# TensorE's certain expert turns written out, their gathered tiles transposed in place

## The reference

```python
logits = x @ router_w + router_b
topv, topi = jax.lax.top_k(logits, TOP_K)              # 2 of 8 experts
topw = jax.nn.softmax(topv, axis=-1)
h1 = jnp.einsum('bsd,edf->ebsf', x, W1) + b1[:, None, None, :]   # 128 -> 512
h2 = jnp.einsum('bsd,edf->ebsf', x, W2) + b2[:, None, None, :]
h = h2 * jax.nn.silu(h1)
eo = jnp.einsum('ebsf,efd->ebsd', h, W3) + b3[:, None, None, :]
return jnp.einsum('bse,ebsd->bsd', comb, eo)           # comb: the two weights
```

## Time and profile before

| | us |
|---|---|
| median of 3 runs (lowest, highest) | 233.26 (233.03, 235.13) |
| the profiled execution, its span | 232.94, 230.7 |
| PE busy | 200.1 (87%) |
| DVE busy | 177.7 (77%) |
| POOL busy | 139.5 (60%) |
| ACT busy | 116.9 (51%) |
| chain that ended last: PE, DVE, issue | 51%, 26%, 10% |

### The profile page before, as it was taken

One profiled execution on the slowest core, in us unless ns is written; L12 is line 12 of the kernel. 1 busy time (PEld: TensorE's weight loads), 2 busy tenths in 40 slices (PEclk: granted clock), 3 DMA queues, 4 the chain that ended last, 5 costly groups with the idle time before them and its releaser, 6 DMA issues.

```text
span 230.7 us, 7408 instructions
## 1 busy us (share of the span) xinstructions
PE 200.1 (87%) x2508; PEld 171.6 (74%) x2510; DVE 177.7 (77%) x411; ACT 116.9 (51%) x378; POOL 139.5 (60%) x247
## 2 busy tenths in 40 slices
PE   6989998999999899999886857859999999999680
PEld 2668887788788778888674247759999888899660
DVE  6178989999999999999966896356766676679064
ACT  2666787788787767886442342222442344442000
POOL 0362566566788888763128486645666766666832
PEclk9999999999999999999996597988999999999978
DMA  5799980000029000001012000111111121215613
GB/s 178 210 255 403 346 234 5 0 4 3 4 72 285 14 3 3 0 4 50 26 50 68 0 0 14 45 35 42 31 45 45 34 43 31 41 34 151 173 66 92
DMA packets 21871, 18.11 MB, mean 78 GB/s; under 512 B 2313, under 2 KB 18770, under 8 KB 21842
## 3 DMA queue, kind: packets, MB, share of 16 engines
q1 hardware_dynamic: 19010, 13.85, 19.9%
q0 software_dynamic: 1280, 2.62, 4.7%
q10 hardware_dynamic: 1552, 1.25, 1.7%
HBM read 12.86 MB, written 4.85 MB: 77 GB/s over the span
## 4 chain that ended last, share of the span: by engine, by line
PE 51%; DVE 26%; issue 10%; DMA 5%; POOL 3%; ACT 2%; DVEq 1%; another core or an unknown queue 0%; POOLq 0%; SPq 0%; ACTq 0%
PE score L867 8%; PE bank L867 7%; PE bank L647 7%; PE bank L878 6%; DVE rsum L1162 5%; PE score L704 5%; DVE smax L1145 5%; PE bank L735 3%; PE bank L742 3%; DVE lo_hot L1363 2%; PE score L700 2%; DVE s_sb L1152 2%; DMA yb<-y_scratch_b 2%; DMA y_scratch_b<-eo_last,row_now 2%; PE bank L954 2%
## 5 line engine op out<-in xcount | busy, mean ns | idle before, releaser
L1145 DVE TENSOR_REDUCE smax<-score 128x16 f32<-128x1024 f32 x24 | 29.0, 1209 | 6.2 <-PE score L704 5.9
L995 ACT ACTIVATE pt_sb<-bank 128x512 f32<-128x512 f32 x48 | 26.1, 594 | 14.0 <-PE bank L647 14.0
L440 POOL TENSOR_TENSOR k<-kt,cst 128x512 f32<-128x512 f32 x24 | 25.2, 1049 | 10.8 <-ACT kt L985 10.4
L1152 DVE TENSOR_TENSOR s_sb<-score,smax 128x1024 f32<-128x1024 f32 x24 | 29.4, 1224 | 0.8
L593 POOL DMA_INDIRECT early<-xm_scratch,tok_i x22 | 22.4, 1018 | 9.6 <-issue 5.7
L704 PE MATMUL score<-k,q 64*128 64x256 f32 x192 | 25.7, 385 | 0.0
L647 PE MATMUL bank<-cst,s_sb 128*128 128x128 f32 x192 | 25.4, 275 | 0.0
L1162 DVE RECIPROCAL rsum<-bank 128x128 f32<-128x128 f32 x24 | 22.9, 954 | 3.2 <-PE bank L742 2.8
L867 PE MATMUL score<-xgt,w_now 128*128 128x128 f32 x160 | 22.9, 303 | 2.3 <-issue 1.6
L867 PEld LDWEIGHTS score<-xgt,w_now 128*128 128x128 f32 x160 | 21.2, 214 | 3.6 <-issue 3.5
L647 PEld LDWEIGHTS bank<-cst,s_sb 128*128 128x128 f32 x192 | 21.3, 140 | 2.4 <-issue 2.3
(11 more groups left out here) (219 smaller groups left out, 430.5 us busy)
## 6 DMA issues: line engine op xcount, KB each, us to landing
w_up<-in_L_ffn_W SPq DMA_DIRECT2D x2, 2048.0 KB, 13.0
w<-in_L_ffn_W SPq DMA_DIRECT2D x8, 256.0 KB, 5.0
y_scratch_a<-zero_row SPq DMA_DIRECT2D x1, 1024.0 KB
y_scratch_b<-zero_row SPq DMA_DIRECT2D x1, 1024.0 KB
xm_scratch<-xm SPq DMA_DIRECT2D x8, 128.0 KB, 2.1
ya<-y_scratch_a SPq DMA_DIRECT2D x4, 256.0 KB, 3.6
early<-in_x SPq DMA_DIRECT2D x1, 512.0 KB, 7.4
early<-in_ctx SPq DMA_DIRECT2D x1, 512.0 KB, 3.3
```

The lines of the kernel that those rows point to most:

```text
L440: g.tensor_tensor(k2[:, n % 3, :, :, :], kt[:, n % 2, :].rearrange("c (b u k) -> c b u k", b=2, u=1).to_broadcast([P, 2, NQ, S]), mask_p.r ...
L995: A(pt_sb[:, b, :], ps_pt[b][:, :], ACT.Exp, scale=SCALE).then_inc(a_pt, 1)
L1145: v.tensor_reduce(smax[:, :, :], score[:, :, :].rearrange("q b (p k) -> q b p k", k=S), AX.X, ALU.max).then_inc(d_mx, 1)
L1152: v.tensor_tensor(s_sb[:, :, :].rearrange("q b (p k) -> q (b p) k", k=S), score[:, :, :].rearrange("q b (p k) -> q (b p) k", k=S), smax[:, ...
```

## The change

PE's turns 0 to 5 are written out one after the other, and the run-time loop covers the rest. For those turns, and for pair 1 ahead of them, PE waits for the gathers itself and transposes the gathered tiles out of `xg`; DVE's copy, with its waits for the gathers and for PE, is left out there. Later turns still copy to `xs`. DVE's, ACT's and POOL's lists are otherwise as they were.

```diff
-            def turn_slots():
+            def turn_slots(tiles):
                 for u in range(2):
-                    k = turn(ps_xgt[:, u * P:(u + 1) * P], xs[:, u, :], ident)
+                    k = turn(ps_xgt[:, u * P:(u + 1) * P], tiles[u], ident)
                 k.then_inc(pe_xgt, 1)
+            def turn_gathered(i):
+                for u in range(2):
+                    pe.wait_ge(g_got[u], 16 * i)
+                turn_slots([xg[:, 2 * i + u, :] for u in range(2)])
...
-            pe.wait_ge(d_xs, 1)
-            turn_slots()
-            def turn_of(i, more):
+            turn_gathered(1)
+            def turn_of(i, sure, more=True):
...
-                if more:
-                    pe.wait_ge(d_xs, i + 2)
-                    turn_slots()
+                if sure:
+                    turn_gathered(i + 2)
+                elif more:
+                    pe.wait_ge(d_xs, i - (SURE - 2))
+                    turn_slots([xs[:, u, :] for u in range(2)])
...
-            with pe.Fori(0, ahead) as i:
+            for i in range(SURE - 1):
                 turn_of(i, True)
-            turn_of(ahead, False)
+            with pe.Fori(SURE - 1, ahead) as i:
+                turn_of(i, False)
+            turn_of(ahead, False, False)
...   (VectorE, ahead of its loop)
-            for u in range(2):
-                dve.wait_ge(g_got[u], 16)
-            take_slots(2)
...   (VectorE, in turn_of)
                 if more:
                     ea, eb = pair_of(i + 2)
+                if more and not kept:
                     for u in range(2):
                         dve.wait_ge(g_got[u], 16 * i + 32)
```

## The result

The changed kernel took 236.21 us in the median of 4 runs (235.07 to 238.09), the kernel before 233.25 (233.03 to 235.13): a ratio of 1.0156, 95% interval 1.0085 to 1.0226. The forecast was 232.3 and no change; it came out slower, above the range's 234.0. Its profiled execution took 235.26 us, with a span of 233.1.

A forecast was written before the change was run, and what follows sets the result against it. It took a circle of POOL's transfers and DVE's late signal, 6.69 us a turn, as the bound; turn 1's scatter(b) about 0.95 us earlier takes the profiled 232.94 to 232.0, plus 0.3 for the median: 232.3; range 229.2 to 234.0.

The forecast's parts named there:

- A turn without a break: PE's expert turn with up, down, transposes and bias products back to back: 5.82 us, against 6.69 in turns 3 to 5.
- The 0.38 us of "issue": PE's gap ahead of up(0) each turn, read as a wait for DVE's `w_now` copy, not the loop's branch.
- the rival of late code: PE's written-out turns: three to four more instruction packets, up to 4.9 us, 237 to 238 us; chance of slower 0.12.
- The copies: DVE's `xs` copies, 0.29 us each, six in the loop and one ahead; from turn 3 on worth nothing.
- the sum's last: From turn 2's end, POOL's series decides and the gain of 0.95 us passes unchanged to turn 6 and the end.
- POOL's series: POOL's four gathers and scatters a turn, issued without a pause, 5.40 us with gaps; keep_out(1) starts 1.89 us after a gather's start.
- the circle: Turns 3 to 5: scatter, gather, keep_out(1), next scatter, in all 6.69 us a turn, with neither PE's loop nor `xs` in it.
- the 0.95: Gain in us at turn 1: POOL's scatter(b) there about 0.95 us earlier.
- the late word: PE's signal that down(1) is done reaches DVE some 2.4 us late, holding keep_out(1); cause not seen in the trace.
- the 0.18 us of the rival: Worth a turn of dropping the `xs` copy if the late signal goes; rival that the circle breaks, 228.6 us, chance 0.27.
- Turn 1's start: Up(0) of turn 1 at 159.4, not 160.52: 1.1 us earlier, between 0.7 and 1.4 by the granted clock.
- the earlier first transposes: Pair 1's transposes ahead of the turns run by 149 without the copy, so turn 0's up(0) comes 1.9 us early.

The follow-up runs named there:

- E2: Kernel before, with only pair 1 transposed out of `xg` ahead of the turns; PE keeps its loop: 224.79 us, ratio 1.0037.
- E8: Kernel before, with DVE's keep_out(1) and ACT's copy of side 0 made by hand to wait for up(1)'s end: 233.21 us, ratio 1.0404.
- E12: E8 with the `w_now` copy put ahead of keep_out(1) in DVE's list: 228.99 us, ratio 1.0213 to the kernel before.
- E1: Kernel before, with PE's turns 0 to 5 written out alone, copies and their waits kept: 225.71 us, ratio 1.0008.
- E3: Changed kernel with pair 1 again through `xs`, turns 0 to 5 still written out: 224.60 us, ratio 0.9993 to the kernel before.
- E6: Changed kernel once more, unchanged, on a later occasion: 225.37 us, ratio 1.0009 to the kernel before.
- E10: Kernel before, with hidden(1) made by hand to wait for the first half of the next up(0): 238.70 us, ratio 1.0679.
- E11: Changed kernel, with hidden(1) made by hand to wait for the first half of the next up(0): 236.05 us, ratio 1.0496 to the kernel before.
- E9: Changed kernel with the same waits added as E8: 229.31 us, ratio 1.0243 to the kernel before.
- E5: Kernel before once more, unchanged, on a later occasion: 224.66 us, ratio 0.9891 for the very same code.
- E14: Changed kernel once more, unchanged, on one more occasion: 225.15 us, ratio 1.0027 to the kernel before.
- E13: Changed kernel with load_up(0), the `w_now` copy, ahead of keep_out(1) in DVE's list: 225.64 us, ratio 1.0048 to the kernel before.

## Why the prediction was wrong

**Right.** A turn without a break was put at 5.82 us and takes 5.80. The 0.38 us of "issue" was a wait for `w_now`, not the loop's branch (E2 keeps the loop and has 5.80 us turns; E8 shows the gap with the releaser's name; E12 removes it). The written-out code cost nothing and brought nothing (E1), three more packets notwithstanding, so the rival of late code is out; in the changed kernel's first trace, too, every idle stretch of PE in turns 1 to 7 ends with keep_out(0), none is put down to "issue". The Trainium skill's page "Runtime: NRT & Kernel Launch", section "Instruction fetch mechanics", says that kernels prefer full unrolling because a taken branch can stall. By the page the stall needs a target outside the fetched window; in E2, whose PE loops over a turn, no turn shows one. The copies were worth nothing while words were on time (E3, E6).

**The step that failed** is the sum's last: "POOL's series decides, and the circle hands the 0.95 on unchanged to turn 6 and the end." I had taken the place of the late word as part of the circle. It moved. In the changed kernel it fell on up(1) or down(0), and so on keep_out(0), which PE's down(1) waits for. PE stood 3.57 us there in turn 1 and 0.67 to 1.59 us in each of turns 3 to 7; of turn 1's 12.07 us, the low clock behind the gap was another 2.5. So the 5.4 us of head start at turn 1 were gone by turn 2, and the turns after it took up to 0.95 us more than before. E10 and E11 give this place its price, 0.9 and 0.8 us a turn over the late word of down(1) in the same kernel. The prediction asked for the price of each late engine ("what is late next") only where the word already was late.

**The circle was also drawn wrong.** "Neither PE's loop nor `xs` is in it": E8 against E9 says that under the late word of down(1) the change saves 0.38 us a turn. The medians differ by 3.9 us, of which turns 0 to 6 of the two traces show 2.3; the rest lies ahead of the turns or behind them. In E8 the `xs` copy stands in DVE's list behind the work that the late word pushes back, and holds the transposes (175.06, right behind the copy); up(1) stands behind these, and the next late word behind up(1). The 0.30 us of E12 are the same wait. Costing it at nothing while the circle stands was wrong, with the 0.18 us of the rival too small by half. And POOL's series did not decide by itself: the same series stands beside words on time in E6. What else made words late is open.

**A term mis-sized.** Turn 1's start: forecast 1.1 us earlier, measured 5.4. Of these, 1.7 lay ahead of anything that the change touches: the prelude's up(1) started at 144.15 and not at 145.82.

The kernel before, then the changed one:

```profile
145.82 2.05 PE L867 MATMUL bank<-xgt,w_now 128*128 128x128 f32 x16
```
```profile
144.15 2.05 PE L873 MATMUL bank<-xgt,w_now 128*128 128x128 f32 x16
```

The stretch before them, 140 to 145, had a granted clock of 0.66 in the kernel before and 1.00 in the changed one. From there to turn 1 the kernel before took 14.7 us and the changed one 11.0; with words on time it is 11.6 (E5) and 10.6 (E6). So the kernel before lost about 3 us there to late words and the low clock that went with them (up(0) took 3.15 us, in E5 2.05), and the changed one, whose hidden(1) started at 146.24 and not 150.44, 0.4. Only about 1.0 was the change's. That this is near the forecast's 1.1 is luck: the forecast took it from the earlier first transposes, and by E2 and E3 it came from the copy left out of turn 0.

**The range** rested on a known wait with an unknown cause. When the trace shows a 2.4 us wait that nothing in it explains, what it does in the changed kernel has no bound from one turn's rows. The prediction gave a slower outcome 0.12 and sought it in the code's fetching; it should have been in the word itself falling on another wait.

**Still open:** why words were late on the first occasion, in both kernels, and in none of the traces taken afterwards, on four chips; and why they fell on up(1) and down(0) after the change and on down(1) before it. Each kernel has one trace of the first occasion, so that it isn't shown that the place belongs to the kernel and not to the single execution. The late words themselves were imitated, not brought back. So that the changed kernel is 1.6% slower is shown for the first occasion only, by its own interval and trace, and from four runs each (E5 shows how far few runs can miss); on two later ones (E6, E14) the intervals hold 1 and nothing beyond 0.7%.

## What to carry to other kernels

A gap marked "issue" is to be checked against the end of every operand's last writer before it is put down to loops or branches. A wait that no row explains is a risk and not a constant: price each place it could fall on, by adding a wait by hand, before trusting a sum. And in an engine's in-order list, work that the critical engine needs soon (here the next weights) should stand ahead of work that waits for that engine's last word: 0.5 us a turn where the word is late (E12), nothing where it is on time (E13).

## What the hardware did unexpectedly

On one occasion DVE and ACT started work that waited only for PE's semaphore some 2 us after PE's matmuls had ended; the trace shows the waiting, and not where the update was held up. Down(1) ended at 175.95 and keep_out(1) started at 178.41; in the changed kernel down(0) ended at 180.22 and keep_out(0) started at 181.99. In the kernel before it goes with 233 us in place of 225: its first trace has about 3 us more than E5's between the prelude's up(1) and turn 1, and 4.5 us more in turns 1 to 7. No edit without a wait added by hand moved a time by as much. In the traces of the later occasions, on four chips, the same kernels had none of it, with POOL's series as dense (E6).
